# Own input products with high and low columns side by side as weights, and selecting matmuls halved, at three quarter boundaries of a four-layer conditioned residual kernel

## What is computed

```
def _lora_linear(x, W, A, B, adapter_indices):
    base = jnp.einsum('bsd,df->bsf', x, W)
    Ai = A[adapter_indices]
    Bi = B[adapter_indices]
    lora = jnp.einsum('bsr,brf->bsf', jnp.einsum('bsd,bdr->bsr', x, Ai), Bi)
    return base + lora
gate = _lora_linear(x, Wg, Ag, Bg, adapter_indices)
up = _lora_linear(x, Wu, Au, Bu, adapter_indices)
h = jax.nn.silu(gate) * up
return _lora_linear(h, Wd, Ad, Bd, adapter_indices)
```

## Time and profile before

| | us |
|---|---|
| median of 3 runs | 1235.41 (1234.34 to 1236.64) |
| the profiled execution, its own time | 1236.46 |
| its span in the trace | 1234.4 |
| TensorE busy | 1223.5 (99% of the span) |
| VectorE busy | 962.9 (78%) |
| ScalarE busy | 568.8 (46%) |
| GpSimd busy | 742.1 (60%) |

### The profile page before, as it was taken

How to read it: one execution, slowest core, us unless ns; L and a number is a source line. 1 busy time by engine, 2 the same in 40 slices (tenths; PEclk the granted TensorE clock), 3 DMA queues, 4 the chain that set the end, 5 groups by cost and what they waited for, 6 DMA issues and landing times.

```text
span 1234.4 us, 18247 instructions
## 1 busy us (share of the span) xinstructions
PE 1223.5 (99%) x6214; PEld 1033.3 (84%) x6214; DVE 962.9 (78%) x1588; ACT 568.8 (46%) x1027; POOL 742.1 (60%) x622
## 2 busy tenths in 40 slices
PE   8999999999999999999999999999999999999998
PEld 7888888888888888888888888888888888888886
DVE  7987787887688787888678778778868877677775
ACT  3744455444544454554344544544534443444333
POOL 4577667648736667656864566675675554444453
PEclk9999999999999999999999999999999999999999
DMA  5866456456875355556496544546659442323423
GB/s 197 287 220 222 139 143 201 138 174 189 272 250 164 108 153 158 169 166 199 147 336 189 177 123 143 170 147 190 199 179 323 150 120 83 91 84 85 112 89 107
DMA packets 141690, 209.60 MB, mean 170 GB/s; under 512 B 44192, under 2 KB 88480, under 8 KB 141600
## 3 DMA queue, kind: packets, MB, share of 16 engines
q1 hardware_dynamic: 117696, 135.45, 35.3%
q0 software_dynamic: 23040, 71.85, 19.5%
q10 hardware_dynamic: 864, 1.15, 0.3%
HBM read 164.36 MB, written 44.04 MB: 169 GB/s over the span
## 4 chain that ended last, share of the span: by engine, by line
PE 95%; DVE 2%; issue 1%; POOL 0%; DMA 0%; another core or an unknown queue 0%; ACT 0%; DVEq 0%; POOLq 0%
PE pd L1770 29%; PE px L1770 28%; PE py L1770 14%; PE pz L1770 7%; PE pz L1787 3%; PE pv L1816 2%; PE pv L1814 2%; PE py L1787 2%; PE px L1787 2%; PE pd L1797 1%; PE px L1921 1%; PE py L1921 1%; PE pd L1906 1%; PE pd L1939 0%; PE pd L2076 0%
## 5 line engine op out<-in xcount | busy, mean ns | idle before, releaser
L813 POOL TENSOR_TENSOR h_lo<-g,h_hi 128x512 fp32r<-128x512 f32 x127 | 183.0, 1441 | 286.5 <-ACT h_hi L961 285.8
L776 POOL DMA_INDIRECT b_got<-b_table,idx_b x192 | 198.4, 1033 | 61.3 <-issue 52.4
L1770 PE MATMUL px<-xo_hi,wg_hi 128*128 128x512 f32 x516 | 207.3, 402 | 1.4 <-DVE wg_lo L1409 0.9
L1543 DVE TENSOR_TENSOR acc<-pd,acc 128x512 f32<-128x512 f32 x248 | 164.3, 684 | 51.3 <-PE pd L1770 50.0
L1770 PE MATMUL px<-xo_hi,wg_lo 128*128 128x512 f32 x516 | 202.5, 392 | 0.0
L1770 PE MATMUL px<-xo_lo,wg_hi 128*128 128x512 f32 x516 | 200.9, 389 | 0.0
L1409 DVE TENSOR_TENSOR wg_lo<-w_raw,wg_hi 128x512 fp32r<-128x512 f32 (+1 forms) x256 | 180.8, 712 | 25.9 <-ACT wg_hi L961 13.7
L1770 PE MATMUL pd<-wd_hi,h_hi 128*128 128x512 f32 x504 | 199.7, 396 | 0.0
L961 ACT ACTIVATE wg_hi<-w_raw 128x512 fp32r<-128x512 f32 (+1 forms) x260 | 146.0, 570 | 112.7 <-PE py L1787 55.1
L1770 PE MATMUL pd<-wd_lo,h_hi 128*128 128x512 f32 x504 | 197.9, 393 | 0.0
L1770 PE MATMUL pd<-wd_hi,h_lo 128*128 128x512 f32 x504 | 196.6, 390 | 0.0
(11 more groups left out here) (337 smaller groups left out, 2504.5 us busy)
## 6 DMA issues: line engine op xcount, KB each, us to landing
w_raw<-w_gu SPq DMA_DIRECT2D x65, 512.0 KB
wd_raw<-w_dn SPq DMA_DIRECT2D x64, 256.0 KB
xo_hi<-xops SPq DMA_DIRECT2D x21, 512.0 KB, 6.1
xo_lo<-xops SPq DMA_DIRECT2D x21, 512.0 KB, 7.1
acc<-x SPq DMA_DIRECT2D x8, 1024.0 KB, 8.8
ad_raw<-ad_table SPq DMA_DIRECT2D x16, 512.0 KB
ad_table<-ad_rows_kept SPq DMA_DIRECT2D x12, 512.0 KB
xops<-st_hi SPq DMA_DIRECT2D x24, 256.0 KB, 2.8
```

The costliest lines, as they stand in the source:

```text
L776: gp.indirect_dma_start(out=dst, out_offset=None, in_=rows_of, in_offset=bass.IndirectOffsetOnAxis(ap=rows.bitcast(U32), axis=0)).then_inc ...
L813: return gp.tensor_tensor(dst, src_raw, src_hi, ALU.subtract)
L1543: ins = dve.tensor_tensor(dst, pd[j][:, :], dst, ALU.add)
L1770: ins = pe.matmul(psum, w_parts[wi], x_parts[xi], start=(start and i == 0), stop=(stop and i == 2), skip_group_check=more)
```

## The change

The own weights are laid out differently: in a run of 128 weight columns stand two samples' 64 high columns and, behind them, their 64 low columns, so that one matmul with the high part of x gives both high by high (in rows 0 to 63 of the bank) and low by high (in rows 64 to 127). The product with the low part of x takes the first 64 columns alone. The moving operand is 128 columns wide (two samples), where it was 256. The two halves of the bank are added when the remainder is taken: `ua_low` becomes two VectorE instructions on 64 rows each, the second behind a wait for the first; `h_hi` then holds the high part in rows 0 to 63 and the remainder in rows 64 to 127, and one matmul of `select` does what two did. The selectors and their pattern are laid out to match. The own high and low parts are taken in two instructions of 256 columns a group, where there was one of 512. `ua_high` is on 64 rows.

```
             t, cp = g // 2, g % 2
-            src = own(cp)[:, 2 * TP * t:2 * TP * (t + 1), :, :].rearrange("p s c e -> p c s e")
-            homes = own_homes(g)
-            return src, parts(homes[0]), parts(homes[1])
+            src = own(cp)[:, 2 * TP * t:2 * TP * (t + 1), :, :].rearrange("p (n s) c e -> p c n s e", s=2)
+            for c, home in enumerate(own_homes(g)):
+                parts = home.rearrange("p (n k s e) -> p k n s e", k=2, n=TP, s=2)
+                yield src[:, c], parts[:, 0], parts[:, 1]
...
-                    src, hi_part, _ = own_group(g)
-                    copy(hi_part, src).then_inc(w_hi_done[g], 1)
+                    for src, hi_part, _ in own_group(g):
+                        ins = copy(hi_part, src)
+                    ins.then_inc(w_hi_done[g], 1)
...
-                copy(h_hi[:, t, m, :], ua_bank(q, t, m)[:, :]).then_inc(ua_hi_done, 1)
+                rows = HC if q else P
+                copy(h_hi[0:rows, t, m, :], ua_bank(q, t, m)[0:rows, :]).then_inc(ua_hi_done, 1)
...
-                    for s in range(HS + 2):
-                        lo, hi = s * SAMPLE_ROWS, min((s + 1) * SAMPLE_ROWS, SEL_COLS)
+                    for s in range(SEL_COLS // SAMPLE_ROWS):
...
-                    src, hi_part, lo_part = own_group(g)
                     dve.wait_ge(w_hi_done[g], n + 1)
-                    dve.tensor_tensor(lo_part, src, hi_part, ALU.subtract).then_inc(w_done[g], 1)
+                    for src, hi_part, lo_part in own_group(g):
+                        ins = dve.tensor_tensor(lo_part, src, hi_part, ALU.subtract)
+                    ins.then_inc(w_done[g], 1)
...
                 dve.wait_ge(ua_hi_done, ua_made(q, t, m))
+                if q:
+                    bank, rest = ua_bank(q, t, 0), up0[HC:P, :]
+                    dve.tensor_tensor(rest, bank[0:HC, :], h_hi[0:HC, t, 0, :], ALU.subtract).then_inc(ua_rest, 1)
+                    dve.wait_ge(ua_rest, 2 * (q - 1) + t + 1)
+                    dve.tensor_tensor(h_hi[HC:P, t, 0, :], bank[HC:P, :], rest, ALU.add).then_inc(ua_done, 1)
+                    return
...
+                        if q:
+
+                            first = c * P % SEL_REPEAT
+                            ins = pe.matmul(select_bank(q, t, m, c), sel_own[:, m, first:first + P], h_hi[:, t, 0, tokens],
+                                            start=True, stop=True)
+                            continue
...
-                    for c in range(2):
-                        for a in range(2):
-                            cols = slice((2 * c + a) * P, (2 * c + a + 1) * P)
-                            tok = slice(c * TOK + a * HALF, c * TOK + (a + 1) * HALF)
-                            for i, (wi, xi) in enumerate(((0, 0), (0, 1), (1, 0))):
-                                ins = pe.matmul(ua_bank(q, t, 0)[:, a * HALF:(a + 1) * HALF], w_parts[wi][:, cols],
-                                                (xo_hi, xo_lo)[xi][:, k, tok], start=(cp == c == a == i == 0),
-                                                stop=True, skip_group_check=True)
+                    bank = ua_bank(q, t, 0)
+                    for c, home in enumerate(own_homes(2 * t + cp)):
+                        for j in range(TP):
+                            tok = slice(j * P, (j + 1) * P)
+                            x_tok = slice(c * TOK + j * P, c * TOK + (j + 1) * P)
+                            pe.matmul(bank[:, tok], home[:, tok], xo_hi[:, k, x_tok], start=(cp == c == j == 0),
+                                      stop=True, skip_group_check=True)
+                            ins = pe.matmul(bank[0:HC, tok], home[:, j * P:j * P + HC], xo_lo[:, k, x_tok],
+                                            start=False, stop=True, skip_group_check=True)
```

More of the change, by code:

```diff
@@ L78 @@
 LAST_ROWS = 2 * TERMS * RANK
-SEL_REPEAT = HS * SAMPLE_ROWS
-SEL_COLS = SEL_REPEAT + P - P // 2
+SEL_REPEAT = 2 * SAMPLE_ROWS
+SEL_COLS = SEL_REPEAT + P - P // 4
+PATTERN_AT = 2 * 2 * TP * SAMPLE_ROWS
 PAIR_ORDER = (0, 4, 1, 5, 2, 6, 3, 7)
@@ L199, in cond_resid_kernel @@
         p_int = small(8).bitcast(I32)
-        pattern_kept = f_one[:, 0:2 * SAMPLE_ROWS].rearrange("p (k n) -> p k n", k=2)
-        slot_mask = f_one[:, 2 * SAMPLE_ROWS:2 * SAMPLE_ROWS + 2 * HS]
+        pattern_kept = f_one[:, 0:SAMPLE_ROWS]
+        slot_mask = f_one[:, SAMPLE_ROWS:SAMPLE_ROWS + 2 * 2]
         ints = eb_one[:, 0, :].bitcast(I32).rearrange("p (a n) -> p a n", a=2)
@@ L349, in cond_resid_kernel @@
         own_mm = sem("own_mm")
+        ua_rest = sem("ua_rest")
         slots_done = sem("slots_done")
@@ L1156, in own_selectors @@
                     act.wait_ge(slots_done, 1)
-                    for s in range(HS + 2):
-                        lo, hi = s * SAMPLE_ROWS, min((s + 1) * SAMPLE_ROWS, SEL_COLS)
-                        at = 2 * (s % HS) + m
-                        ins = act.activation(sel_own[:, m, :, lo:hi], pattern_kept[:, :, 0:hi - lo], ACT.Copy,
+                    for s in range(SEL_COLS // SAMPLE_ROWS):
+                        at = 2 * (s % 2) + m
+                        ins = act.activation(sel_own[:, m, s * SAMPLE_ROWS:(s + 1) * SAMPLE_ROWS], pattern_kept, ACT.Copy,
                                              scale=slot_mask[:, at:at + 1])
@@ L1690, in _ @@
                     dve.wait_ge(layer_mm, QP)
-                    dve.tensor_copy(pattern_kept, pattern)
-                    for at in range(2 * HS):
-                        ins = dve.tensor_scalar(slot_mask[:, at:at + 1], p_f[:, 0:1], float(at), None, ALU.is_equal)
+                    for half in range(2):
+                        rows = slice(half * HC, (half + 1) * HC)
+                        dve.tensor_copy(pattern_kept[rows, :], pattern[rows, half, :])
+                        for at in range(2 * 2):
+                            ins = dve.tensor_scalar(slot_mask[rows, at:at + 1], p_f[rows, 0:1], float(2 * 2 * half + at),
+                                                    None, ALU.is_equal)
                     ins.then_inc(slots_done, 1)
@@ L1898, in select @@
                     for m in range(2):
-                        for part, ua in enumerate((h_hi, h_lo)):
[L1900 to L1906, removed]
+                        if q:
[3 more added lines that the diff above has]
+                            continue
+                        for part, ua in enumerate((h_hi, h_lo)):
+                            ins = pe.matmul(select_bank(q, t, m, c), sel[:, part, c * P:(c + 1) * P], ua[:, t, m, tokens],
+                                            start=(part == 0), stop=(part == 1))
                 ins.then_inc(sel_mm, 1)
```

9 lines of the change are left out of this document (3 added, 6 removed).

## The result

The changed kernel takes 1239.56 us (median of 7 runs, 1238.10 to 1240.38), the kernel before 1234.83 us in the same comparison: a ratio of 1.0035, 95% interval 1.0026 to 1.0044, that is 3.2 to 5.4 us more. The forecast was 1239.4 us, 4.0 us more than the median of 1235.41 us that it started from.

A forecast was written before the change was run, and what follows sets the result against it. At each boundary, VectorE's chain through `ua_low(q, 1)`, not the 99% busy TensorE, was taken to set S2's start. A11 of block 1 comes +1.35 us late, 3 x 1.35 = 4.0 us, so 1239.4 us; range 1235.5 to 1242.0.

The forecast's parts named there:

- `ua_low` in two costs 0.80 us each: VectorE at each boundary: two dependent 64x512 instructions take 1.41 us instead of 0.61, +0.80 each time, upper +0.88.
- The lower bound, +0.61: `ua_low` on VectorE: two instructions at 0.61 us each, so +0.61 us instead of +0.80.
- Own parts in halves, 0.41 us late: ACT and VectorE before `add_down(q - 1, 7, 1)`: 256-column instructions add 0.12, 0.14 and 0.15 us.
- the forecast +1.75 us at S2: Block 0's third product: `ua_low(q, 1)` starts 0.95 us late and takes 0.80 more, so S2 is +1.75 late.
- `ua_high(q, 1)` waits for ACT's folds and not for the own products: ACT at the boundary: it follows `ea_one` and `eb_one`, starting at 344.24 instead of 343.27; earlier own products buy nothing.
- The 0.67 us of `select(q, 0)` becomes idle time: TensorE ahead of A11: the 0.67 us saved is idle, since A11 waits for `ua_done` until about 346.3.
- Block 1 is held by the silu, and gets 0.4 of the 0.67 us back: A11 of block 1 waits for ACT's silu and starts +1.35 us late, where S2 is +1.75 late.
- The own products, 0.09 us a matmul: TensorE's 32 own matmuls at about 0.09 us, 2.8 us in all; ends 0.06 (1.9 us) and 0.11 (3.5 us).
- Faster because TensorE's saving counts: Rival: slack before S2 or cheap `ua_low` halves let TensorE's saving count, 1231.4 us or 1225.7; chance 0.08.
- Nearly earned back: Rival: `ua_low` at its lower bound and block 1 held by TensorE, +0.7 us a boundary, 1237.5 us; chance 0.22.
- Nothing of either shows: Rival: delays and saved matmuls cancel to within 0.3 us a boundary; chance 0.03.
- dear short matmuls: Rival: own matmuls at the upper price give 1240.6 us, at 0.22 us each 1261.6; chance 0.07 above the range.

The follow-up runs named there:

- b_ua_pair: Kernel before, with only `ua_low` from quarter 1 on cut into two VectorE instructions of 64x512, the second waiting for the first: 1238.81 us against 1235.37, ratio 1.0032.
- b_own_halves: Kernel before, with only the own high and low parts taken in two instructions of 256 columns a group: 1235.20 us against 1235.37, ratio 0.9998.
- a_sel0_12: Changed kernel, with each of the 6 matmuls of `select(q, 0)` issued twice: 1239.45 us against 1235.37 for the kernel before, ratio 1.0036.
- a_act_sel: Changed kernel, `keep_s1` of block 0 ahead of `v_high(q - 1, 1)`, `select(q, 0)` ahead of `v_mask(q - 1, 1)`: 1238.98 us against 1235.16 for the kernel before.
- a_pool: Changed kernel, with `v_mask(q - 1, 1)` moved from VectorE to GpSimd: 1236.16 us against 1235.16 for the kernel before, ratio 1.0007.
- a_all: Changed kernel, `v_mask(q - 1, 1)` on GpSimd, `keep_s1` ahead of `v_high`, three VectorE low parts later: 1233.28 us against 1235.16; again 1233.66, ratio 0.9988.
- b_all: Kernel before, all matmuls as before, with the same reordering and move to GpSimd as a_all: 1234.14 us, ratio 0.9993.
- a_all2: As a_all, with GpSimd's gathers ahead of the last `v_mask` instruction, `v_high` and `v_low` later: 1235.50 us against 1235.53 for the kernel before.
- a_all3: As a_all2, with VectorE's low part of group 3 ahead of `finish(q - 1, 0)`: 1235.06 us against 1235.14 for the kernel before, ratio 0.9997.
- b_all2: Kernel before, matmuls as before, with the same reordering as a_all2: 1235.39 us, ratio 0.9994 to the kernel before.

## Why the prediction was right

The direction, the size and the way were as forecast: +4.0 us forecast, +3.2 to +5.4 measured, 3.85 by the three boundaries of the trace. That the medians lie within 0.2 us of each other is partly luck: the own parts were priced 0.26 us a boundary too dear, an unforeseen 0.2 us at the third boundary made up for some of it, and the kernel before has a median of 1234.83 us over its seven runs where the forecast started from 1235.41. Point by point:

- *`ua_low` in two costs 0.80 us each.* It costs 0.84 (1.45 for 0.61). The second starts 0.03 us behind the end of the first, and the instruction behind the pair 0.04 us behind its end, the upper case of the forecast. (The forecast compares 1.41, taken to the end of the pair, with 0.61, taken to the next start; from start to start its rows give +0.72, and +0.83 for the upper case, which is what was measured.) The lower bound, +0.61, and with it the rule of the Trainium skill, "VectorE: DVE Perf Modes", section "The DRAIN you can't avoid", that a semaphore between two instructions costs nothing extra, do not hold here: the next instruction starts 0.08 us before the end of the one ahead if it does not wait for it, and 0.03 us behind it if it does. A wait on another engine that is long over costs nothing: the fold at 344.51 has one and starts 0.08 us early. The same fold behind the pair, whose second half is on rows 64 to 127, starts 0.04 us late in the changed kernel and in b_ua_pair, so there it is the other rows that cost and not a wait. b_ua_pair shows that this one term carries the whole loss.
- *Own parts in halves, 0.41 us late.* Mis-sized: it costs nothing (b_own_halves). I had passed the 0.26 us of groups 0 and 1 on in full, through `v_mask` and `v_high`, and overlooked that a fold of 0.40 us work took 0.70 us there, held by GpSimd. With 0.26 us off, the forecast +1.75 us at S2 becomes +1.49; measured +1.52.
- *`ua_high(q, 1)` waits for ACT's folds and not for the own products.* Right: it follows `eb_one` without a gap, 1.3 us behind the start of the last own matmul at 340.48, so that the own products end earlier is worth nothing (timeline of ACT, changed kernel):

```profile
341.50 0.40 ACT L962 ACTIVATE eb_one<-vacc 64x256 f32<-64x256 f32 x1
341.81 0.57 ACT L962 ACTIVATE h_hi<-px 64x512 fp32r<-64x512 f32 x1
```

- *The 0.67 us of `select(q, 0)` becomes idle time.* Right, and shown by a_sel0_12: putting the matmuls back moves A11 by 0.0 us.
- *Block 1 is held by the silu, and gets 0.4 of the 0.67 us back.* 1.52 - 1.21 = 0.31 us comes back. Right in kind, and 0.4 was a little much; that VectorE's sum of work is a chain of its own is shown by a_act_sel and a_pool.
- *The own products, 0.09 us a matmul.* 0.17 us for two: 0.11 us with 128 weight columns and 0.06 with 64, 2.69 us in all. So neither of my ends is the rule: the wide ones cost no less than with 192 moving columns, the narrow ones half. The estimate of 2.6 us that the prediction also gives came within 0.1 us; the mean of 84 ns a matmul hides the two prices.
- *Faster because TensorE's saving counts.* Fell: TensorE is busy 3.0 us less and stands idle 6.4 us at the boundaries. *Nearly earned back* fell too: the pair takes 1.45 us and not the 1.22 of its lower bound, and block 1 is held by the silu. *Nothing of either shows* fell with the 1.2 to 1.4 us a boundary, *dear short matmuls* with 2.69 us an own product.
- Not foreseen: the wait of 0.5 to 0.7 us ahead of `select(q, 0)`, for VectorE's addition from `pv`. It costs nothing by itself, since A11 behind it waits for VectorE anyway.
- Not foreseen: the third boundary is 0.2 us longer than the other two, in this and two other runs of kernels with the new products, and not in all. The delay is there before any new product runs: ScalarE's first own high part starts 2.98 us ahead of the first own product, where the other two boundaries have 3.21. I have not found why.

## What to carry to other kernels

Before taking work off the busiest engine, find at each place of the edit which engine sets its next start; here, at S2 behind each boundary, a 99% busy TensorE came no more than 0.1 us ahead of VectorE's chain, so halving its selecting matmuls was worth 0.3 us of 1.35, and each VectorE instruction that was cut in two cost up to 0.8. An edit that moves cost to the engine that runs just behind needs that engine's order redone with it: with GpSimd's idle time used and three instructions put later, the same products give 1233.3 and 1233.7 us, about 0.1% less than the kernel before (both ratios are given above) and some 0.4% less than the changed kernel. How much of that is due to the new products stays open by the times: a_all and b_all, the same order with the new and the old ones, are 0.9 us apart, and their intervals overlap. The traces put it a little higher: at boundaries where TensorE waits for no gather, A11 of block 1 stands at 27.20 to 27.26 with the new products and at 27.78 with the old, 0.5 us a boundary.

## What the runs showed of the hardware

- A VectorE instruction that takes both its inputs from SBUF is held while GpSimd runs a two-input instruction: with 256 columns it ends 0.29 to 0.30 us behind GpSimd's end in the kernel before (0.70 us for 0.40 us of work), in a_all2 (1.16 for 0.42), in a_all3 (0.73 and 1.06) and in b_all2 (1.91). With 512 columns it ends 0.55 us behind (kernel before: `g<-g,up` at 325.63 takes 1.41 us, to 327.04, and GpSimd's instruction ends at 326.49). Additions from PSUM beside the same GpSimd instruction were not stretched (four in 2.47 us). In these places the profile shows it as a long instruction, not as idle time.
- A VectorE instruction starts 0.08 us before the end of the one ahead of it, but 0.03 us behind that end if it waits for it, and 0.04 us behind it where the one ahead was on rows 64 to 127 and it is on rows 0 to 63.
- By the distance to the next start, a matmul of 128 moving columns takes 0.11 us with 128 weight columns and 0.06 us with 64 (0.17 us for the two, alternating), where 256 moving columns take 0.12 us with 128 and 0.11 to 0.12 with 64.
- Two profiled executions differed by 1.43 us through a single wait in the first 20 us; comparing their spans alone would have given less than half of this change's cost.
